# A four-part kernel that sets its semaphores back: most clears moved from the blocks between the parts into the parts

## The reference, cut to what matters

```python
x = x + _L0_attn_a_ref(_layernorm(x, axis=-1), ...)   # latent attention, 16 heads, causal
x = x + _L0_ffn_ref(_layernorm(x, axis=-1), L0_ffn_weight, L0_ffn_scale)
x = x + _L0_attn_b_ref(_layernorm(x, axis=-1), ...)   # cosine attention, 16 query heads, one key head
x = x + _L0_ffn_ref(_layernorm(x, axis=-1), L0_ffn_weight, L0_ffn_scale)
x = x + _L1_attn_a_ref(_layernorm(x, axis=-1), ...)   # gated linear attention
x = x + _L1_ffn_ref(_layernorm(x, axis=-1), ...)      # workspace of 16 slots, two rounds
x = x + _L1_attn_b_ref(_layernorm(x, axis=-1), ...)   # attention with adapters
x = x + _L1_ffn_ref(_layernorm(x, axis=-1), ...)
return x
```

## Time and profile before

| what | us |
|---|---|
| median of 3 runs | 2129.46 |
| lowest, highest | 2122.96, 2131.7 |
| the profiled execution's own time | 2129.9 |
| its span, first to last instruction | 2128.0 |
| of it busy: PE 1949.6, DVE 1019.8, ACT 808.2, POOL 520.4 | 92%, 48%, 38%, 24% |

### The profile page before, as it was taken

One profiled execution on the slowest core, in us unless ns is written; L12 is line 12 of the kernel. 1 busy time (PEld: TensorE's weight loads), 2 busy tenths in 40 slices (PEclk: granted clock), 3 DMA queues, 4 the chain that ended last, 5 costly groups with the idle time before them and its releaser, 6 DMA issues. The chain is left out here.

```text
span 2128.0 us, 30267 instructions
## 1 busy us (share of the span) xinstructions
PE 1949.6 (92%) x11630; PEld 1251.8 (59%) x11630; DVE 1019.8 (48%) x2232; ACT 808.2 (38%) x1780; POOL 520.4 (24%) x621
## 2 busy tenths in 40 slices
PE   7999999999899999999999999968977799999884
PEld 5556666565566767676677666723354444545652
DVE  3555556545323234333333322279975665546443
ACT  2543444545333223332342234224423234445342
POOL 2322232323111011101010100035642243542221
PEclk9999999999999999999999999989989999999988
DMA  5000000000010000000000000020000000000001
GB/s 230 1 1 1 1 1 1 1 1 1 5 73 1 1 1 1 1 1 1 1 1 1 1 1 1 1 71 1 0 1 1 1 1 1 2 1 2 1 1 40
DMA packets 9774, 24.03 MB, mean 11 GB/s; under 512 B 2449, under 2 KB 6305, under 8 KB 8865
## 3 DMA queue, kind: packets, MB, share of 16 engines
q1 hardware_dynamic: 8336, 18.92, 2.4%
q10 hardware_dynamic: 1296, 3.18, 0.4%
HBM read 20.00 MB, written 2.10 MB: 10 GB/s over the span
## 5 line engine op out<-in xcount | busy, mean ns | idle before, releaser
L1489 PEld LDWEIGHTS cos_ps<-cos_vx,cos_probs 128*128 128x128 f32 x2048 | 238.7, 191 | 33.6 <-issue 28.7
L1489 PE MATMUL cos_ps<-cos_vx,cos_probs 128*128 128x129 f32 x2048 | 239.8, 275 | 4.2 <-DVE cos_on L1171 4.2
L1480 PE MATMUL cos_ps<-lead_room,cos_kT 128*128 128x512 f32 x512 | 233.5, 600 | 8.5 <-PEq L50 6.1
L1362 ACT ACTIVATE cos_probs<-cos_ps 128x512 f32<-128x512 f32 x256 | 150.7, 598 | 161.9 <-PE cos_ps L1480 160.7
L671 ACT ACTIVATE probs<-sc,nmax 128x512 f32<-128x512 f32 (+3 forms) x256 | 132.5, 525 | 168.0 <-DVE nmax L525 165.9
L1273 POOL TENSOR_TENSOR cos_qrs<-cos_qse,neg_half 128x4 f32<-128x4 f32 x59 | 59.5, 1008 | 488.4 <-DVE cos_qse L1153 488.4
L780 PE MATMUL sc<-kT,qT 128*128 128x512 f32 (+3 forms) x512 | 170.6, 455 | 4.8 <-DVE probsT L537 2.5
L1480 PEld LDWEIGHTS cos_ps<-lead_room,cos_kT 128*128 128x128 f32 x512 | 95.3, 192 | 110.7 <-issue 104.7
L2959 DVE TENSOR_REDUCE cos_wq<-tail_ps 128x2 f32<-128x1024 f32 (+3 forms) x128 | 101.7, 823 | 80.7 <-PE tail_ps L3199 79.7
L1151 DVE TENSOR_REDUCE cos_qss<-cos_qsq 128x4 f32<-128x512 f32 x59 | 40.5, 686 | 189.2 <-ACT cos_qsq L1341 189.2
L752 PE MATMUL pq<-xnT,wap 128*128 128x512 f32 x256 | 123.9, 606 | 1.5 <-DVE swp L517 1.5
(11 more groups left out here) (495 smaller groups left out, 3431.7 us busy)
## 6 DMA issues: line engine op xcount, KB each, us to landing
onT<-in_mla_wqT SPq DMA_DIRECT2D x1, 2048.0 KB, 9.5
lead_room<-in_mla_wo SPq DMA_DIRECT2D x1, 2048.0 KB, 19.8
cos_wq<-in_cos_wq SPq DMA_DIRECT2D x1, 2048.0 KB, 25.7
cos_wout<-in_cos_wout SPq DMA_DIRECT2D x1, 2048.0 KB, 7.5
out<-x SPq DMA_DIRECT2D x4, 512.0 KB, 2.9
x<-in_x SPq DMA_DIRECT2D x1, 1536.0 KB, 15.0
wq_pe<-in_mla_wq_pe ACTq DMA_DIRECT2D x1, 1024.0 KB, 14.6
x<-in_x SPq DMA_DIRECT2D x1, 512.0 KB, 4.4
```

The lines of the kernel that those rows point to most:

```text
L1362: act.activation(probs[:, n % 2, kj, :], ps[:, kj, :], ACT.Exp).then_inc(s["e_done"], 1)
L1480: pe.matmul(ps[:, kj, :], kT[:, b % 2, kj * P:(kj + 1) * P], qT[:, hq % 2, h % 4, :], start=True, stop=True).then_inc(s["s_ready"], 1)
L1489: last = pe.matmul(po[:, qi // 2, qi % 2, :], probs[:, n % 2, kj, qi * P:(qi + 1) * P], vx[:, b % 2, kj, :], start=(kj == 0), stop=(kj == ...
```

## The change

A list `cleared` in `Kit`, and `clear_done(engine, sems)`, which clears the given semaphores on the given engine inside a part; `clear_sems` leaves those out. SyncE does it in all four parts, behind a wait that says that the semaphores are no longer used; ScalarE clears those of "second" at the end of its list in part four. The semaphore `stored` of the output transfers becomes one of the whole kernel's, and three others that count loads (`weights_loaded`, `late_loaded`, `last_loaded`), which were not cleared before, are cleared in part three.

```diff
+    def clear_done(self, engine, sems):
+        for s in sems:
+            engine.sem_clear(s)
+        self.cleared += sems
 
     def clear_sems(self):
             @block.gpsimd
             def _(pool):
                 for s in self.sems:
-                    pool.sem_clear(s)
+                    if not any(s is c for c in self.cleared):
+                        pool.sem_clear(s)
...
                 for dst, src, done in g["early_loads"]:
                     sp.dma_start(dst, src).then_inc(done, 16)
+                sp.wait_ge(g["weights_loaded"], 16 * len(g["early_loads"]))
+                sp.wait_ge(s["o_ready"], PAIRS)
+                k.clear_done(sp, [s[n] for n in names if n not in ("o_ready", "o_done", "y_ready", "x_done")])
...
                 for dst, src, done in loads:
                     sp.dma_start(dst, src).then_inc(done, 16)
+                sp.wait_ge(s["ta_done"], 2 * TI * B)
+                sp.wait_ge(s["td_done"], 2 * TI * B)
+                k.clear_done(sp, [s[n] for n in names if n not in ("ta_done", "td_done", "y_ready", "y_var", "y_rstd", "y_done")])
...
                 sp.wait_ge(loaded, 16 * len(loads))
+                sp.wait_ge(s["ogT_ready"], 2 * B)
+                k.clear_done(sp, [s[n] for n in names if n not in ("ogT_ready", "filled", "emptied_v", "emptied_a", "st_ready", "ws_rstd",
+                                                                   "ws_msq")]
+                             + [g["weights_loaded"], g["late_loaded"], loaded])
...
             def _(sp):
+                sp.wait_ge(stage["second"]["s"]["xb_ready"], 1)
+                k.clear_done(sp, list(stage["first"]["s"].values()) + list(stage["lora"]["s"].values()))
                 stage["second"]["by_sync"](sp)
...
                 for name in ("first", "lora", "second"):
                     stage[name]["by_scalar"](act)
+                k.clear_done(act, [sem for n, sem in stage["second"]["s"].items()
+                                   if n not in ("xb_ready", "m2_ready", "r2_ready", "sums_scaled", "x_ready", "x_added")])
```

More of the change, by code:

```diff
@@ L35, in __init__ @@
         self.nc, self.ctx = nc, ctx
-        self.sems = []
+        self.sems, self.cleared = [], []
     def sb(self, name, shape, dtype=F32):
@@ L2189, in workspace_programs @@
              "a_ready", "a_copied", "at_ready", "ash_ready", "ae_ready", "att_ready", "pt_ready", "attT_ready",
-             "xb_ready", "m2_ready", "r2_ready", "x_ready", "stored", "sums_scaled", "x_added")
+             "xb_ready", "m2_ready", "r2_ready", "x_ready", "sums_scaled", "x_added")
     s = {n: k.sem(f"{tag}_{n}") for n in names}
@@ L2212, in by_sync @@
             sp.dma_start(out[b, :, :].rearrange("(i p) d -> p i d", p=P), x[:, tiles(b), :])\
-              .then_inc(s["stored"], 16)
-        sp.wait_ge(s["stored"], 16 * B)
+              .then_inc(g["stored"], 16)
+        sp.wait_ge(g["stored"], 16 * B)
     def statistics(dve, b):
@@ L3215, in free_left @@
             pe.wait_ge(s[left[n][0]], left[n][1])
-    return {"by_vector": by_vector, "by_gpsimd": by_gpsimd, "by_scalar": by_scalar, "by_tensor": by_tensor,
+    return {"s": s, "by_vector": by_vector, "by_gpsimd": by_gpsimd, "by_scalar": by_scalar, "by_tensor": by_tensor,
             "row_stats": row_stats, "norm_rows": norm_rows, "invert": invert, "masked_adapters": masked_adapters,
@@ L3316, in _ @@
                     stage[name]["by_tensor"](pe)
+        k.sems.append(g["stored"])
         k.clear_sems()
@@ L3442, in build @@
              "ws_eps": k.sb("ws_eps", [P, TI])}
-        for n in ("weights_loaded", "late_loaded", "last_loaded"):
+        for n in ("weights_loaded", "late_loaded", "last_loaded", "stored"):
             g[n] = k.sem(n)
```

## The result

| kernel | median us | lowest to highest | runs |
|---|---|---|---|
| before | 2126.13 | 2122.96 to 2131.7 | 5 |
| after | 2107.27 | 2106.18 to 2114.14 | 5 |

The ratio is 0.9918, with a 95% interval of 0.9893 to 0.9943. The changed kernel is 0.8% faster, and its median lies 1.7 us under the forecast of 2109.0 and inside the range. The forecast was reckoned from a median before of 2129.46, three runs; over five runs that median is 2126.13, so that the saving between the medians is 18.9 us where 20.5 was forecast. The profiled execution of after took 2112.59 us, with a span of 2110.9.

A forecast was written before the change was run, and what follows sets the result against it. GpSimd's four runs of clears were taken to lie wholly on the path. Savings of 16.7 (clears), 2.8 and 1.0 us (TensorE's clock), together 20.5, gave 2109.0 us against a median of 2129.46; range 2103.5 to 2116.5.

The forecast's parts named there:

- Clears, 16.7 us (16.3 to 17.2): At the four blocks behind the parts: 229 clears leave GpSimd's path at 0.071 us each, saving 16.7 us.
- break: In three of GpSimd's four clear runs: one pause some 0.3 us longer than a step, 0.9 us together, perhaps kept.
- Added clears and waits, nothing: In all four parts: clears moved to SyncE and ScalarE, and their waits, are hidden and cost nothing.
- the covers: At the parts' ends: time hiding moved clears; late from 0.27, 0.47, 0.24, 0.86 (SyncE) and 0.21 us each (ScalarE).
- The bound of 0.43 us: On SyncE: issuing a transfer, taken as its dearest instruction, sets the most that a moved clear could cost.
- the slower rival: On SyncE and ScalarE: dear clears delay the barriers, up to 2137 us at 0.43 us each; chance 0.04.
- No other wait in the block's place: At the seams: denies the rival that bare code fetches replace the blocks, about 2121 us, chance 0.06.
- Clock behind part one, 2.8 us: At part two's start: shorter TensorE idleness keeps its clock at 2.4 GHz, saving 2.8 us, chance about three in four.
- Clock behind part two, nothing: At part three's start: 9.1 us of idleness stay, so the clock stays low; 0, between -1 and +1 us.
- Clock behind part three, 1.0 us (0 to 3.0): At part four's start: TensorE idleness shrinks from 3.57 to 1.9 us, giving back 1.0 us of slow-clock time.
- The sum, 20.5: Whole kernel: removed clears 16.7 plus clock gains 2.8 and 1.0 us make 20.5 us saved.
- clears alone: Whole kernel, rival: only the removed clears count, clock gains fail or are lost elsewhere; 2112.8 us, chance 0.30.

The follow-up runs named there:

- e2: Changed kernel with part one's 63 clears put back on GpSimd, the rest as changed; median 2115.46 us, ratio 0.9941 to before.
- e5: Changed kernel with every moved clear issued five times in a row; median 2123.02 us, ratio 0.9971 to before.
- e3: Kernel before plus 80 dummy products on TensorE while GpSimd clears behind part one; median 2126.10 us, ratio 0.9994 to before.
- e7: Changed kernel plus 125 dummy products at the end of TensorE's list of part two; median 2105.39 us, ratio 0.9894 to before.
- e1: Kernel before with only part four's clears moved, to SyncE and ScalarE; median 2120.76 us, ratio 0.9958 to before.
- e6: Changed kernel run once more with no edit; median 2105.52 us, ratio 0.9899 to before.
- e8: e7 plus 120 dummy products on a zeroed tile ahead of TensorE's first work; median 2111.39 us, ratio 0.9922 to before.
- e4: Kernel before with one ranged clear per run of neighbouring semaphores, 5 instead of 253, all on GpSimd; median 2109.83 us, ratio 0.9906 to before.
- e10: The same code as e4, run again; median 2108.59 us, ratio 0.9907 to before.

## Why the prediction was right

*Clears, 16.7 us (16.3 to 17.2).* The blocks shrank by 17.09 us, near the upper bound: none of the four blocks of after holds a break. That is luck of position. The breaks stand 128 instructions of GpSimd's list apart, or multiples of that (e2), and taking clears out shifts all that follow; in e2 two blocks of 6 and 7 clears hold one each. So 16.3 us is the gain of the removed steps and the rest, up to 0.9, goes by where the breaks fall.

*Added clears and waits, nothing.* Right. Of the covers, those of part one and of ScalarE were sized rightly (e5); that of part three holds only where its last products run at the lower clock, and is 4.6 us instead of 6.3 where they don't. The assumed step of 0.071 us was above what SyncE needs: 3.3 us over 58 steps is 0.057, 4.5 over 70 is 0.064; ScalarE's 2.9 over 45 is 0.064. The bound of 0.43 us was misread as the dearest issue of a transfer on SyncE: one at 591.81 takes 0.85 (line 1060), so that the slower rival reached further than the prediction says. It changes nothing, with a step of 0.06. The Trainium skill, page "Runtime: NRT & Kernel Launch", section on the preamble and postamble, gives 51 semaphores in 1.5 us, by which one would take 0.03, an estimate. SyncE's recorded durations, mostly 0.025 to 0.030 us, agree with it, but the step from one to the next, which is what a list costs, is twice that.

*No other wait in the block's place.* Right. SyncE is released at 575.7 and TensorE's first product starts at 575.83. Counted from GpSimd's release it starts 0.16 us later at the first two seams and 0.31 at the third, each time as in before.

*Clock behind part one, 2.8 us.* It measured 2.85, by the idle stretch of 1.60 us with the clock at 1.00 behind it; e2 takes it away and e3 gives it without the clears. Over the other executions it is a little less: part two took 814.3 to 814.8 us with the long seam ahead of it and 811.9 to 812.1 with a short or a filled one. The Trainium skill, page "TensorE: Matmul & The Clock Gate", section "HAM oscillation", puts the cold start down to long gaps between bursts; the trace agrees here, and behind part three only in part, as the next but one paragraph shows.

*Clock behind part two, nothing.* Right: 8.85 us of idleness stay, and the same activation stands 13.14 us into the part before and 13.15 after. e7 shows that 0.95 was there to be had.

*Clock behind part three, 1.0 us (0 to 3.0).* From TensorE's first product of part four to ScalarE's first exponential of the workspace is 1595.43 - 1580.10 = 15.33 us before, 1581.01 - 1566.93 = 14.08 after, and 1585.16 - 1572.08 = 13.08 in e2. Before, after, e2:
```profile
1595.43 0.72 ACT L2457 ACTIVATE room<-wsp_lt,wsp_ntop 128x512 f32<-128x512 f32 x1 [2.41 <-DVE wsp_ntop L2269]
```
```profile
1581.01 0.72 ACT L2474 ACTIVATE room<-wsp_lt,wsp_ntop 128x512 f32<-128x512 f32 x1 [2.42 <-DVE wsp_ntop L2286]
```
```profile
1572.08 2.84 PE L2516 MATMUL tail_ps<-ident,cos_wq 128*128 128x128 f32 x24 [1.94 <-DVEq L2372]
1585.16 0.72 ACT L2471 ACTIVATE room<-wsp_lt,wsp_ntop 128x512 f32<-128x512 f32 x1 [2.41 <-DVE wsp_ntop L2283]
```
```profile
1572.00:1585.20 13.20, 11.40 (x154) 9.34 (x155) 6.81 (x28) 4.76 (x10) 3.54 (x5) 1.00 0.01 1
```
The last row is a window of e2 with a granted clock of 1.00. So the difference was 1.25 us in after, and 2.25 where the clock doesn't fall at all. But the 1.25 is not the change's for certain: e3, which leaves this block and its idle stretch of 3.57 us as before, also took 14.08 us, with the fall 1 us into the part. e5 aside, the three executions with the long stretch took 15.33, 15.22 (e1) and 14.08 us, the eight with the short one 14.08 (three of them) or 13.08 (five): in the mean 14.9 and 13.5, a term of 1.4 us.

The idle stretch is the same in after and e2, 1.95 and 1.94 us. Whether a fall comes behind a stretch of this length is then not set by the stretch alone: one came in after, e6 and e8, none in e2 and e7, where the block is as long. Over all seams, no fall followed within 5 us on the eleven idle stretches of 1.60 to 1.72 us, and one did on four of the seven of 1.87 to 1.95.

*The sum, 20.5.* The terms as these two executions show them measure 17.09 + 2.85 + 1.25 = 21.2 us; with the two clock terms as the means over all executions (814.5 less 811.9 in part two, and the 1.4 above) it is 21.1. The two profiled executions differ by 17.1, because chance took 4.1 back: part one -3.52, part three +1.71, the rest of part four 4.65 + 1.25 = +5.90. The medians, over more executions, differ by 18.9. The rival "clears alone" forecast 2112.8; its mechanism, that the clock gives nothing back at the seams, is refuted by e2 and e3, though its second half, that shifted work meets falls elsewhere, is what one sees in a single execution.

*What the chance is made of.* In part four, eleven executions (all but e5) lie on a line of 0.35 us for each us at 1.2 GHz (correlation 0.93), from 535.03 us with 42.9 at the lower clock to 543.40 with 64.2. In part three two places show whole. At one, eight products of the output projection behind an idle stretch of 3.1 us take 1.99 us, or some 3.6 where the clock falls just then. Before, after, e3:
```profile
1481.99 1.99 PE L2030 MATMUL gla_ps<-gla_wo,cos_wout 128*128 128x256 f32 x8 [3.12 <-DVE x L1736]
```
```profile
1468.76 3.68 PE L2047 MATMUL gla_ps<-gla_wo,cos_wout 128*128 128x256 f32 x8 [3.13 <-DVE x L1753]
```
```profile
1475.64 3.60 PE L2036 MATMUL gla_ps<-gla_wo,cos_wout 128*128 128x256 f32 x8 [3.12 <-DVE x L1742]
```
At the other, the last 16 products of the projection take 5.38 or 3.69 us. Before, then e2, and after is as before (5.38 us from 1559.61):
```profile
1571.14 5.38 PE L2030 MATMUL gla_ps<-gla_wo,cos_wout 128*128 128x256 f32 x16 [2.77 <-DVE cos_wout L1729]
```
```profile
1566.45 3.69 PE L2044 MATMUL gla_ps<-gla_wo,cos_wout 128*128 128x256 f32 x16 [2.65 <-DVE cos_wout L1743]
```
Before is slow at the last place alone, e2 and e3 at the first alone, and all three took 175.9 us. After, e6 and e8 are slow at both and took 177.3 to 177.6. So the 1.71 us between before and after are the first place, 3.68 against 1.99. It is slow in e3 too, whose part three and the block ahead of it are those of before, and of e4 and e10, which are the same code, e4 is slow at the last place alone and e10 at the first. These falls come and go with no edit.

Part one differs at its very start. The same products as in the fence of after under e8, before:
```profile
17.30 13.75 PE L723 MATMUL sc<-lead_room,onT 128*128 128x64 f32 x64
30.84 1.92 PE L746 MATMUL sc<-ident,kc 128*128 128x128 f32 x8
```
The 64 products took 13.75 us and not 7.80; in after TensorE then waited 4.32 us for VectorE where it waited 1.52 before, so not all of it counts. Which of the two it is goes with no edit: e4 and e10 have the long start, e2, e3 and e6 the short one; e3's part one is the code of before and took 575.07 us, 3.5 less.

What stays open is why a fall comes at one place and not at another in equal code. I have shown where falls land and what they cost, and not what sets them. In before, idle stretches of TensorE between 2.7 and 4.0 us had a fall within 2.2 us of their end in seven of eight cases, those between 1.2 and 2.4 us in two of fifteen; but falls also come while it works, and after and e6 share theirs from 1468 to 1714 and differ behind it by 7.8 us.

## What to carry to other kernels

A block between two parts in which one engine works and four wait is on the path whole, however small its busy time looks; measure it from barrier to barrier, by the step between instructions and not by their recorded length. Work of that kind can go under the tail of the part ahead, on an engine that has finished early, and its cover is the distance from the wait that frees it to the barrier, divided by the number of instructions; take it with the work ahead of the barrier at the high clock, since at the low one it looks longer than it will always be (e5). But first ask whether fewer instructions do the same, as the ranged clear did here without touching any part. A shorter idle stretch of TensorE can give its clock back behind it; count that in the stretch behind the seam alone, and don't read single profiles that differ by less than what falls of the clock elsewhere move.

## What the runs showed of the hardware that I had not expected

- One clear of a range of 63 neighbouring semaphores took 0.378 us on GpSimd, of 36 0.223 and of 30 0.199: some 5.4 ns for a semaphore and 28 to 37 ns beside, against 0.071 us for each when cleared singly.
- The step between clears differs by engine: 0.057 to 0.064 us on SyncE, 0.064 to 0.069 on ScalarE, 0.071 on GpSimd.
- In a run of clears, one instruction in 128 of the engine's list starts some 0.3 us late, at places that are fixed in the list: on GpSimd in before (324, 452, 1092), on SyncE in e5 (79, 207, and on to 975), on ScalarE in e5 (2111, 2239).
- 120 products kept TensorE busy up to 9.8 us, and yet the clock fell at 18.6, behind an idle stretch of 2.35 us, and stayed low to 32.3 although TensorE worked without a pause from 17.08 to 29.61 (e8).
- The profile's granted clock says nothing at a program's start: its first record in before is at 33.1 us, and the windows show 1.00 ahead of it, while 8 products of 128x128 (line 746) took 1.92 us there, and 1.04 us in after (line 756).
- Equal code took 535.6 and 543.4 us in part four. A single profiled execution of this kernel is good to some 8 us as a whole, and to 0.1 us in a stretch where the clock is equal.
